# A graph layer with eight experts: from the third chunk on, VectorE makes the router's logits from the normalised rows

## The reference

```python
x = x + gnn(xn, edge_index, ...) + mix(xn[None], ...)[0]
xr = layernorm(x)                       # the "normalised rows" of this text
w = softmax(xr @ Wr + br)               # router: 256 -> 8, for each row
h = relu(bn(einsum('bfd,edh->bfeh', xr, W1) + b1))
h = relu(bn(einsum('bfeh,ehk->bfek', h, W2) + b2))
y = einsum('bfeh,ehd->bfed', h, Wo) + bo
x = x + einsum('bfed,fe->bfd', y, w)
```

## Time and profile before

| | |
|---|---|
| time, median of 3 runs | 1103.9 us (1102.42 to 1104.52) |
| profiled execution, span from first to last instruction | 1101.4 us |
| profiled execution, its own time | not recorded apart from the span |
| TensorE busy | 1092.1 us (99%), weight loads 979.2 (89%) |
| VectorE busy | 752.0 us (68%) |
| ScalarE busy | 735.4 us (67%) |
| GpSimd busy | 247.1 us (22%) |

### The profile page before, as it was taken

The page is one execution under the profiler, slowest core; times in us unless marked ns, Lnnn a source line. Parts: engine busy times, 40 slices in busy tenths (PEclk is TensorE's granted clock), DMA queues, the critical chain, the costliest instruction groups (busy, mean ns, idle before and its releaser), DMA issues.

```text
span 1101.4 us, 19301 instructions
## 1 busy us (share of the span) xinstructions
PE 1092.1 (99%) x6656; PEld 979.2 (89%) x6656; DVE 752.0 (68%) x1752; ACT 735.4 (67%) x1275; POOL 247.1 (22%) x287
## 2 busy tenths in 40 slices
PE   9999999999999999999999999999999999999998
PEld 7988988989888888888898888888888988889998
DVE  7888756776576675775765766757657657666565
ACT  5777757775675766666756757666667566666665
POOL 4787753312012021030120120210301201100000
PEclk9999999999999999999999999999999999999999
DMA  6877851211011110110110111101101101100000
GB/s 187 262 233 253 233 187 34 59 40 49 1 50 49 39 49 11 39 59 1 49 49 6 45 49 39 50 11 39 59 1 49 49 12 33 35 20 1 1 21 15
DMA packets 71300, 67.92 MB, mean 62 GB/s; under 512 B 20641, under 2 KB 66579, under 8 KB 71203
## 3 DMA queue, kind: packets, MB, share of 16 engines
q1 hardware_dynamic: 66552, 59.34, 17.8%
q0 software_dynamic: 3968, 6.71, 2.4%
q10 hardware_dynamic: 683, 0.64, 0.2%
HBM read 40.87 MB, written 25.80 MB: 61 GB/s over the span
## 4 chain that ended last, share of the span: by engine, by line
PE 92%; POOL 3%; issue 2%; DVE 2%; ACT 1%; DMA 0%; DVEq 0%; POOLq 0%; ACTq 0%
PE bank L280 29%; PE bank L281 28%; PE bank L282 28%; PE bank L985 1%; POOL gathered L597 1%; PE bank L1152 1%; PE bank L1164 1%; PE bank L1162 1%; PE bank L926 1%; PE bank L918 1%; PE bank L1180 0%; POOL gathered L615 0%; POOL alpha_l L617 0%; PE bank L942 0%; DVE sum_squares L1337 0%
## 5 line engine op out<-in xcount | busy, mean ns | idle before, releaser
L1381 DVE SCALAR_TENSOR_TENSOR accumulated<-bank,router_w,accumulated 128x256 f32<-128x256 f32 (+2 forms) x392 | 170.4, 479 | 199.3 <-PE bank L282 192.8
L661 ACT ACTIVATE h<-weight_stage 128x512 fp32r<-128x512 f32 (+2 forms) x206 | 113.5, 598 | 196.8 <-PE bank L282 177.4
L282 PE MATMUL bank<-ffn_w_high,h 128*128 128x256 f32 (+2 forms) x778 | 220.0, 283 | 0.0
L280 PE MATMUL bank<-ffn_w_high,h 128*128 128x256 f32 (+2 forms) x778 | 219.7, 282 | 0.2 <-DVE h L1231 0.2
L281 PE MATMUL bank<-ffn_w_low,h 128*128 128x256 f32 (+2 forms) x778 | 219.9, 283 | 0.0
L1231 DVE TENSOR_TENSOR h_low<-activated,h_high 128x512 fp32r<-128x512 f32 (+2 forms) x208 | 135.3, 657 | 79.4 <-ACT h_high L661 75.7
L812 ACT ACTIVATE activated<-bank,bn_cols 128x512 f32<-128x512 f32 (+2 forms) x208 | 156.3, 751 | 48.5 <-PE bank L282 45.1
L812 ACT ACTIVATE weight_stage<-bank,bn_cols 128x512 f32<-128x512 f32 (+2 forms) x208 | 154.2, 751 | 47.7 <-PE bank L282 46.2
L280 PE MATMUL bank<-xT_high,ffn_w_high 128*128 128x512 f32 (+2 forms) x416 | 159.5, 383 | 0.1
L280 PE MATMUL bank<-h_high,ffn_w_high 128*128 128x512 f32 (+2 forms) x416 | 157.8, 379 | 0.0
L281 PE MATMUL bank<-xT_low,ffn_w_high 128*128 128x512 f32 (+2 forms) x416 | 157.3, 378 | 0.0
(11 more groups left out here) (226 smaller groups left out, 1940.0 us busy)
## 6 DMA issues: line engine op xcount, KB each, us to landing
x_rows<-in_x SPq DMA_DIRECT2D x18, 512.0 KB, 4.8
x_turned<-xT_high SPq DMA_DIRECT2D x22, 256.0 KB, 3.6
x_turned<-xT_low SPq DMA_DIRECT2D x22, 256.0 KB, 4.5
out<-accumulated SPq DMA_DIRECT2D x11, 512.0 KB, 3.3
mix_xT_high<-x_turned SPq DMA_DIRECT2D x10, 512.0 KB
mix_xT_low<-x_turned SPq DMA_DIRECT2D x10, 512.0 KB
weight_stage<-in_L_ffn_W SPq DMA_DIRECT2D x16, 256.0 KB, 3.0
node_table<-gathered SPq DMA_DIRECT2D x22, 132.0 KB, 2.9
```

Of the source, the lines that this page charges most:

```text
L280: nc.tensor.matmul(dst, ah, bh, start=(k == 0), stop=False)
L282: last = nc.tensor.matmul(dst, al, bh, start=False, stop=(k == n - 1))
L661: return nc.scalar.activation(dst, src, ACT.Copy)
L1381: last = V.scalar_tensor_tensor(a, y_of(ch, e)[b][0:tp, (t % 2) * D:(t % 2 + 1) * D], wts(ch)[0:tp, t, e:e + 1], a, ALU.mult, ALU.add)
```

## The change

For the chunks from the third on (`by_rows`: `ch.c >= 2`) TensorE has no `router`. VectorE makes the logits instead: for each tile and each expert one `tensor_tensor_reduce`, which multiplies the tile's 256 normalised columns with one column of `Wr` (laid as a row over all partitions in `wrb`) and sums them. `route_rows` does tile 0 in step 4, tile 1 in step 5, tiles 2 and 3 in step 6. `route_sums` in step 7 adds the bias and subtracts the largest logit. `x2_norm` moves ahead of `hid2` in step 4, `router_exp` from step 6 to step 7, `weights` behind `hid2` in step 7, TensorE's `router_turn` behind `L2` of step 0, and ScalarE's `router_turned` behind `relu2` of step 0. Two transfers are added in the preparation, and two tensors in SBUF, for which `brow` lies inside another tensor and the scratch for GpSimd's transfers is set to 8192.

```diff
+                if i == 20:
+                    sp.dma_start(wr_d, I["L0_ffn_Wr"].rearrange("c e -> e c"), allow_slow_non_contiguous=True).then_inc(s["wr_t"], 16)
+                if i == 30:
+                    need(sp, s["wr_t"], 16)
+                    sp.dma_start(wrb[:, :, :].rearrange("p e c -> p (e c)"),
+                                 wr_d.rearrange("e c -> (e c)").partition_broadcast(P)).then_inc(s["ld_wr"], 16)
...
ScalarE, inside the loop over e
+                    if nxt is not None and by_rows(nxt) and e == NE - 1:
+                        router_exp(nxt)
-                    if e == 0 and ch.c > 0:
+                    if e == 0 and ch.c > 0 and not by_rows(ch):
                         router_turned(ch)
                     relu2(ch, e)
-                    if e == 0 and ch.c == 0:
+                    if e == 0 and (ch.c == 0 or by_rows(ch)):
                         router_turned(ch)
...
TensorE, inside the loop over e
-                    if e == 0 and ch.c > 0:
+                    if e == 0 and ch.c > 0 and not by_rows(ch):
                         router_turn(ch)
                     L2(ch, e)
+                    if e == 0 and by_rows(ch):
+                        router_turn(ch)
...
-                    elif nxt is not None and e in FRONT and not (ch.c == 0 and e == 3):
+                    elif nxt is not None and e in FRONT and not (ch.c == 0 and e == 3) and not (by_rows(nxt) and e == 6):
                         FRONT[e](nxt)
...
VectorE
+            def route_rows(ch, tiles):
+                tp = ch.tp
+                need(dve, s["fx2n"], ch.c + 1)
+                need(dve, s["ld_wr"], 16)
+                for t in tiles:
+                    if t < ch.nt:
+                        for e in range(NE):
+                            n = NE * (ch.g0 - CHUNKS[2].g0 + t) + e
+                            need(dve, s["frr"], n - 1)
+                            last = V.tensor_tensor_reduce(prod[0:tp, e % 2, :], xn[0:tp, t, :], wrb[0:tp, e, :], 1.0, 0.0,
+                                                          ALU.mult, ALU.add, rl[0:tp, t, e:e + 1]).then_inc(s["frr"], 1)
...
+            ROWS_AT = {4: (0,), 5: (1,), 6: (2, 3)}
...
                     if nxt is not None and e == NE - 1:
-                        weights(nxt)
+                        if by_rows(nxt):
+                            route_sums(nxt)
+                        else:
+                            weights(nxt)
+                    if nxt is not None and by_rows(nxt) and e == 4:
+                        x2_norm(nxt)
                     if not (ch.last and e == NE - 1):
                         hid2(ch, e)
+                    if nxt is not None and by_rows(nxt) and e == NE - 1:
+                        weights(nxt)
...
+                        if by_rows(nxt) and e in ROWS_AT:
+                            route_rows(nxt, ROWS_AT.get(e, ()))
```

More of the change, by code:

```diff
@@ L155, in build @@
         onesf = sb("ones", [P, P])
-        brow = sb("kv_bias_row", [P, 2 * D])
         bo3 = sb("bo_rows", [P, TPC, D], f32r)
@@ L196, in build @@
         rhr = sb("router_high", [P, TPC, NE], f32r)
+        wrb = sb("router_rows", [P, NE, D])
+        prod = sb("router_products", [P, 2, D])
         bnr = sb("bn_rows", [4 * NE, 5, P])
@@ L320, in h2_free, with by_rows @@
                 need(eng, s["y"], NE * ch.b0 + ch.nb * e)
+        def by_rows(ch):
+            return ch.c >= 2
         def gathered(ch):
@@ L903, in _ @@
                         relu1(nxt, 0)
-                    if e == 0 and ch.c > 0:
+                    if nxt is not None and by_rows(nxt) and e == NE - 1:
+                        router_exp(nxt)
+                    if e == 0 and ch.c > 0 and not by_rows(ch):
                         router_turned(ch)
                     relu2(ch, e)
-                    if e == 0 and ch.c == 0:
+                    if e == 0 and (ch.c == 0 or by_rows(ch)):
                         router_turned(ch)
-                    if nxt is not None and e in FRONT and not (nxt.c == 1 and e in (0, 2)):
+                    if nxt is not None and e in FRONT and not (nxt.c == 1 and e in (0, 2)) and not (by_rows(nxt) and e == 6):
                         FRONT[e](nxt)
@@ L1394, in small @@
             def small(ch, key):
-                return Chain(dve, s["dsm"], NTILES + PER * ch.c + OFF[key])
+                fewer = sum(by_rows(c) for c in CHUNKS[:ch.c]) + (key == "weights" and by_rows(ch))
+                return Chain(dve, s["dsm"], NTILES + PER * ch.c + OFF[key] - fewer)
             def base_rows(ch):
@@ L1494, in x2_low, with route_sums @@
                     low(xTl[:, ch.par, k, 0:ch.rows], Fb[k][:, 0:ch.rows], xTh[:, ch.par, k, 0:ch.rows]).then_inc(s["f2lo"], 1)
+            def route_rows(ch, tiles):
[9 more added lines that the diff above has]
+                                                          ALU.mult, ALU.add, rl[0:tp, t, e:e + 1]).then_inc(s["frr"], 1)
+            def route_sums(ch):
+                tp, nt = ch.tp, ch.nt
+                sm = small(ch, "route")
+                need(dve, s["frr"], NE * (ch.g0 - CHUNKS[2].g0 + nt))
+                a = rl[0:tp, 0:nt, :]
+                sm.step(V.tensor_tensor(a, a, brbc[0:tp, :].unsqueeze(1).broadcast_to([tp, nt, NE]), ALU.add))
+                sm.step(V.tensor_reduce(rq[0:tp, 0, 0:nt], a, AX.X, ALU.max))
+                V.tensor_tensor(a, a, wide(rq[0:tp, 0, 0:nt], [tp, nt, NE]), ALU.subtract).then_inc(s["flg"], 1)
             def route(ch):
@@ L1585, in _ @@
                     if nxt is not None:
-                        for step in (FRONT_1 if nxt.c == 1 else FRONT).get(e, ()):
+                        for step in (FRONT_1 if nxt.c == 1 else FRONT_R if by_rows(nxt) else FRONT).get(e, ()):
                             step(nxt)
+                        if by_rows(nxt) and e in ROWS_AT:
+                            route_rows(nxt, ROWS_AT.get(e, ()))
             accumulate(LAST, NE - 1)
```

9 lines of the change are left out of this document (7 added, 2 removed).

## The result

The changed kernel takes 1140.7 us (median of 4 runs, 1139.07 to 1141.9) against 1103.45 of the kernel before (4 runs). The ratio is 1.0334, with an interval of 1.032 to 1.0349: 37 us slower. The forecast was 1140.

The account below looks back on a forecast made before the run. TensorE, busy 1092.1 of 1101.4 us, was taken as the bound. Ten full chunks at +3.27 (+32.7), +2.3 for the last and +0.5 for the preparation gave 1136.9, plus 2.5 to the median 1139.5, say 1140; range 1128 to 1195.

Parts of the forecast that it names:

- gain of 18.4 us: TensorE in the main loop: removing the router's matmuls saves 1.71 us in ten chunks, 1.28 in the last.
- price of a product: VectorE's pitch p per product with its sum: 0.424 us, low end 0.334, forecast range 0.39 to 0.46.
- 16p - 4.33: Length of TensorE's wait at the next chunk's L2, from product pitch p, while VectorE is on time at hid2(6).
- first wait: TensorE at the next chunk's first L2 waits for expert 7's relus, queued behind the exp: 2.45 us a chunk.
- second form: Same wait at L2 if steps 4 and 5 make VectorE late: 32p - 11.4, holding from p = 0.44 on.
- Rivals 1 and 2: Sum's read waits, product pitch 0.51 to 0.60, 1165 to 1195 us, chance 0.28; half rate, 0.69, 1226, chance 0.06.
- rival 3: Products don't reach TensorE, only the two fixed waits do: +0.8 us a chunk, 1114 us, chance 0.09.
- rival 5: No change in time, all terms cancelling by chance; chance 0.02.
- second wait: TensorE at router_turn, behind L2 of step 0, waits for VectorE's weights, now behind hid2(7): 0.9 us a chunk.
- The third: TensorE at out_bias in step 0 waits for ScalarE's copy of the turned weights, behind high2: 1.63 us a chunk.
- Rival 4: Copy of turned weights is done before L3(7) ends, so no wait at out_bias: faster, 1085.5 us, chance 0.03.
- The preparation: SP's added transfers before the main loop, SP being ahead of its readers: +0.5 us, bounds 0 to 4.

Follow-up runs that it names:

- all_moves: Changed kernel with Wr turned via SBUF, weights ahead of hid2, exp behind step 7's relus, turned-weights copy ahead of step 0's copies: 1083.23 us, 0.9816.
- strided: Changed kernel without the turn of Wr, spread as it lies, each product reading every eighth number: 1199.1 us, 1.0858.
- copy_early2: Changed kernel with ScalarE's copy of the turned weights between the relus and the high-half copies of step 0: 1122.43 us, 1.0172.
- turn_sbuf: Kernel before, plus the turning transfer of Wr into eight SBUF partitions, unread, and scratch at 8192: 1103.22 us, 0.9994.
- turn_only2: Kernel before, plus only the turning transfer of Wr from DRAM into DRAM, with nothing reading it: 1119.26 us, 1.0149.
- late_load2: Changed kernel with both added transfers moved from the preparation behind the first loads of chunk 0's step in the main loop: 1135.36 us, 1.0287.

## Why the prediction was right, and where it wasn't

**The gain of 18.4 us was real.** all_moves, with every stall gone, is 20.0 faster. A chunk is 1.84 shorter where 1.71 was forecast; the 0.13 more is about the 0.1 by which the first matmul behind the router was late, which the prediction had seen and not counted.

**The price of a product was too high.** The step was "it is nearest to the plain one: p = 0.334 + 0.09 = 0.424". The first term was right to 0.012. The second was wrong: the read of the sum lies beside the next product, which the prediction had named as its low end. So p lies outside the forecast's own 0.39 to 0.46, and "I am wrong if p isn't near 0.42" came true. The formula 16p - 4.33 gives 1.2 for 0.346, and 1.03 was measured. Thus the formula was good to 0.2 and its input wasn't: the first wait was forecast at 2.45, 1.4 too much a chunk. The second form fits for a large p (strided). Rivals 1 and 2 (p from 0.51 up) are out by the pitch, rival 3 by the wait at `L283`, rival 5 by the ratio.

The Trainium skill, "VectorE: DVE Perf Modes", section "The DRAIN you can't avoid", says that the next operation doesn't start before the pipe is empty, and adds that one which isn't held starts earlier. The prediction took only the first half. The changed kernel's trace goes with the second: products that last 0.42 start 0.346 apart. The pitfall of the Trainium skill in "Vector Engine (DVE) Microarchitecture Reference", section "Points that are easy to get wrong", half the throughput for the scalar-tensor-tensor form with two SBUF sources that aren't bf16, isn't seen in these products: half rate would be near 0.60. Whether they are of that form, no row says.

**The second wait** was forecast at 0.9 and measured at 0.78. From the relu's start to the turned matmul were 4.49 us, forecast 4.44. The missing 0.1 is TensorE's own way there, forecast at 3.56 and now 3.71, since `L2` takes 2.89 behind the wait instead of 2.75. **The third** was forecast at 1.63 and measured at 1.63. Rival 4, that the copy would be done in time, is out: it becomes true only when the copy is moved (copy_early2). Each wait could be removed by itself while the others stayed or nearly so, so they add up, as forecast.

**The main loop:** -1.84 + 1.03 + 0.78 + 1.63 = +1.60 a chunk, and some 0.1 after each of the three waits makes it 1.9; measured were 1.99, against the 3.27 of the forecast. Ten of them leave 22.1 - 19.9 = 2.2 for the last chunk, forecast 2.3. Forecast in all +35.0, measured +22.1.

**The preparation is the step that failed:** "SP is ahead of its readers there, so I take +0.5, with 0 to 4 as bounds". It costs 15.1. I had priced the issue of the transfer, by the earlier trace rows, and the issue is indeed 0.74. What costs is what stands behind it in the queue, while it drains: 12.0 us for the next two issues, and `node_table` and its readers behind that. The row I took the bound from moves 512 single numbers into SBUF, and turn_sbuf shows that this direction is nearly free; I had carried its price over to DRAM. It was also where the clock gave way, against "I add nothing for it". The windows of the changed kernel show it behind 14.5 idle us, while the main loop keeps 1.00 through its gaps of up to 1.5:

```profile
102.00:106.00 4.00, 4.00 (x14) 3.45 (x15) 2.56 (x6) 2.68 (x7) 0.35 (x1) 0.50 1.09 383
106.00:110.00 4.00, 4.00 (x24) 3.63 (x23) 2.92 (x10) 2.63 (x6) 3.31 (x3) 0.84 1.07 361
```

At 0.50 and 0.84 these eight microseconds lose about 2.6 (estimate), so the wait and the clock are 17.1 in this execution. It is the slowest of the four (1141.9, 1.2 above the median), which explains more than half of the distance to the 15.1 by the medians.

An error of -12.9 in the main loop (22.1 for 35.0) and one of +14.6 in the preparation (15.1 for 0.5) all but cancel. The time of 1140 was right by luck, by their sum and not by its working: with the main loop as it was and the preparation within its bounds of 0 to 4, the time would have been 1125 to 1129, and 1126 with the 0.5 that was taken, under the lower end of the range (1128).

The Trainium skill, "DMA: Bandwidth & Descriptors", section "Specifications", asks for at least 512 B in a transfer for full rate, and names read-modify-write below it. The runs agree that four bytes at a time can be dear (+15.9 in turn_only2), but only for one of the two destinations tried: the same pieces into SBUF cost nothing (1103.22). Whether read-modify-write is the reason, no run shows.

## What to carry to other kernels

Moving work off the full engine paid what was removed once nothing waited (20.0 us, where the pitch had promised 18.4). What decided was where three small followers stood in their queues: an exp ahead of relus that TensorE needs, weights behind a bulk operation, and a copy behind work that waits for its reader's neighbour. Look through each in-order queue for a late input ahead of something urgent before judging such a trade. And a one-time transfer of a few KB can cost two thirds of what the change cost the whole main loop (15.1 and 22.1 us): price what it does to the queue behind it, in the direction in which it goes.

## What the hardware showed beyond the forecast

- The read of a sum out of VectorE (84 ns) lies beside the next product; 16 pairs took 5.53 us. With every eighth number of one source (32 bytes apart) the same product has a pitch of 0.57 instead of 0.346.
- Moving 2048 single numbers from DRAM into DRAM cost 15.9 us by itself (14 to 18); into SBUF 0 (0.9994, 0.9984 to 1.0004). In the main loop it kept the DMA engines 99% busy at 15 GB/s for 10 us and held up TensorE and ScalarE without a semaphore between them, for reasons that stay open.
- TensorE's granted clock stayed at 1.00 through three gaps of 0.6 to 1.5 us in each chunk, and was 0.50 for some 3 us after a gap of 6.5. In late_load2, where gaps of 2.44, 2.52 and 1.04 us came with little work between them, it was 0.50 from 214 to 221 us.
